# The experts' SiLU written with a hyperbolic tangent in a two-layer kernel on one core

## The reference, cut to what matters

```python
scores = softmax(x @ gate_w); topk_w, topk_idx = top_k(scores, 2)
topk_w = topk_w / (sum(topk_w) + 1e-20)          # w_per_expert: these, spread over the 8 experts
for e in range(8):
    hid = silu(x @ w_gate[e]) * (x @ w_up[e])    # silu(g) = g * sigmoid(g); 128 -> 256 columns
    y = y + w_per_expert[:, e:e+1] * (hid @ w_down[e])
shared = silu(x @ ws_gate) * (x @ ws_up) @ ws_down
return y + shared
```

## Time and profile before

| | us |
|---|---|
| median of 3 runs | 1997.63 (1995.62 to 1999.28) |
| the profiled execution, whole | 1997.42 |
| its span, first to last instruction | 1995.6 |
| TensorE busy / VectorE busy / ScalarE busy | 1638.1 / 1146.3 / 986.9 |
| mean granted TensorE clock | 0.914 of 2.4 GHz |
| ScalarE: ACT_TABLE_LOAD | 100 loads of 1.283 us |

### The profile page before, as it was taken

The page is one execution under the profiler, slowest core; times in us unless marked ns, Lnnn a source line. Parts: engine busy times, 40 slices in busy tenths (PEclk is TensorE's granted clock), DMA queues, the critical chain, the costliest instruction groups (busy, mean ns, idle before and its releaser), DMA issues.

```text
span 1995.6 us, 32820 instructions
## 1 busy us (share of the span) xinstructions
PE 1638.1 (82%) x11632; PEld 956.7 (48%) x11632; DVE 1146.3 (57%) x2565; ACT 986.9 (49%) x2277; POOL 605.0 (30%) x396
## 2 busy tenths in 40 slices
PE   2666569899699978999699978999688988998579
PEld 1334235555446444464546544454445555455235
DVE  6543357557484576557494566646574585744614
ACT  1435253844547544754447535664538445662042
POOL 2624071605242061613324051512515051510000
PEclk9787679999899998999799998999899998999689
DMA  4010011011300122001410123001310123002201
GB/s 131 19 24 1 0 44 41 21 38 44 86 21 2 46 57 65 21 30 32 93 29 5 38 65 64 22 22 32 85 30 21 38 60 68 22 17 61 64 2 53
DMA packets 37333, 80.57 MB, mean 40 GB/s; under 512 B 6782, under 2 KB 22654, under 8 KB 33776
## 3 DMA queue, kind: packets, MB, share of 16 engines
q1 hardware_dynamic: 37152, 78.22, 15.6%
HBM read 54.74 MB, written 8.78 MB: 32 GB/s over the span
## 4 chain that ended last, share of the span: by engine, by line
PE 54%; DVE 16%; ACT 15%; issue 9%; POOL 5%; DMA 1%; DVEq 0%; SPq 0%; POOLq 0%; ACTq 0%
PE ps L350 47%; ACT work L766 8%; PE ps L355 6%; DVE cmax L1116 4%; ACT big L846 4%; POOL small L1237 2%; DVE small L1004 1%; DVE fxn L917 1%; POOL frs L1237 1%; POOL work L1262 1%; DVE x L1198 1%; DVE work L972 1%; POOL work L1273 1%; DVE fst L904 1%; DVE work L971 1%
## 5 line engine op out<-in xcount | busy, mean ns | idle before, releaser
L1262 POOL TENSOR_TENSOR work<-work 128x1024 f32<-128x1024 f32 x64 | 151.0, 2359 | 462.1 <-DVE work L972 461.6
L350 PE MATMUL ps<-bxt,mw 128*128 128x512 f32 x576 | 278.2, 605 | 8.2 <-DVE big L1210 8.2
L350 PE MATMUL ps<-maskb,identb 128*128 128x128 bf16 (+1 forms) x1152 | 237.1, 249 | 47.2 <-ACT work L766 28.2
L766 ACT ACTIVATE work<-ps,pbias,small 128x128 f32<-128x128 f32 x512 | 228.8, 528 | 53.5 <-DVE pbias L1008 53.1
L355 PE MATMUL ps<-ident,work 128*128 128x128 f32 x1056 | 175.2, 313 | 62.7 <-ACT work L766 40.2
L1116 DVE TENSOR_REDUCE cmax<-ps 128x1 f32<-128x384 f32 (+3 forms) x352 | 199.5, 631 | 24.8 <-PE ps L350 24.6
L1237 POOL TENSOR_TENSOR small<-small,consts 128x8 f32<-128x8 f32 x128 | 208.2, 1640 | 5.0 <-DVE small L981 5.0
L350 PE MATMUL ps<-wqkv,h 128*128 128x512 f32 x384 | 188.1, 623 | 23.7 <-ACT v L726 12.0
L1293 POOL TENSOR_TENSOR work<-work,prec 128x1024 f32<-128x1024 f32 x64 | 134.3, 2099 | 209.9 <-DVE prec L999 209.9
L846 ACT ACTIVATE big<-ps 128x512 f32<-128x512 f32 x320 | 167.7, 638 | 58.1 <-PE ps L350 57.8
L868 ACT ACTIVATE big<-ps 128x512 f32<-128x512 f32 x144 | 85.2, 596 | 210.3 <-PE ps L350 209.4
(11 more groups left out here) (163 smaller groups left out, 2600.9 us busy)
## 6 DMA issues: line engine op xcount, KB each, us to landing
mw<-in_experts SPq DMA_DIRECT2D x72, 384.0 KB, 3.1
pk<-scr_parts SPq DMA_DIRECT2D x48, 192.0 KB
pq<-scr_parts SPq DMA_DIRECT2D x144, 64.0 KB
v<-v SPq DMA_DIRECT2D x16, 512.0 KB, 4.5
v<-v SPq DMA_DIRECT2D x16, 384.0 KB, 6.2
scr_parts<-big SPq DMA_DIRECT2D x8, 768.0 KB, 3.7
xin<-in_x SPq DMA_DIRECT2D x8, 256.0 KB, 3.4
out<-x SPq DMA_DIRECT2D x8, 256.0 KB, 6.0
```

What stands on the lines that cost most here:

```text
L350: return nc.tensor.matmul(o, a, b, start=start, stop=stop, skip_group_check=True)
L766: i = nc.scalar.activation(pr[:, m, a, p, :], fb[2 * (m % 2) + a][:, p * P:(p + 1) * P], ACT.Exp, bias=pbias[:, m, k:k + 1], scale=rn[:, m ...
L1262: nc.gpsimd.tensor_tensor(qk[:, m, :], qk[:, m, :], part[m % 2], ALU.add).then_inc(l_add.sem, 1)
```

## The change

The gate's function becomes a tangent on ScalarE. `silu` then holds tanh(g/2). A new step on VectorE, `moe..s`, makes (tanh + 1) · g out of it, in place, from the same PSUM bank. This is twice SiLU. The factor of a half is moved to where it costs no instruction: the sum of the two routing weights is doubled before its reciprocal is taken (one instruction with two operations in place of one), and the shared expert's output is halved in its addition. The semaphore `m_silu` is split into `m_tanh` (ScalarE to VectorE) and `m_gated` (VectorE to TensorE and to its own product), so that a gate's bank is now freed by VectorE. The strings for TensorE, ScalarE and VectorE are new. GpSimd's and SyncE's stay.

```diff
-    "tensor": "FBFBFFFFFFFFFFFFFBBBBFBBBBBBBBBBBBFBBFBBBFBFBBBFFBBBBFBBBBFBBBFBBFBBBFBBBBFBBBBFBBBBBBBBBBBBBBBBBFBB"
+    "tensor": "FFBBFFFFFFFFFFFFFBBBBFBBBBBBBBBBBBFBBBFBBFFBFBBBFBBBBFBBBBFBBBFFBBFBBBBBBBFBBBBFBBBBBBBBBBBBBBBFBFBBF"
...
-        m_silu, m_hid, m_sum = sig("m_silu", ALL * 2), sig("m_hidden", ALL * 2), sig("m_sum", ALL)
+        m_tanh, m_gated = sig("m_tanh", ALL * 2), sig("m_gated", ALL * 2)
+        m_hid, m_sum = sig("m_hidden", ALL * 2), sig("m_sum", ALL)
...
-                                freed = m_hid if q % 2 else m_silu
+                                freed = m_hid if q % 2 else m_gated
...
-                        nc.scalar.activation(silu[e % 2][:, c, :], bb[n % 3][:, :], ACT.Silu).then_inc(m_silu.sem, 1)
+                        nc.scalar.activation(silu[e % 2][:, c, :], bb[n % 3][:, :], ACT.Tanh, scale=0.5).then_inc(m_tanh.sem, 1)
...
-                ts(rs1[:, 3, :], rs1[:, 3, :], 1e-20, None, ALU.add).then_inc(bv.sem, bv.one())
+                ts(rs1[:, 3, :], rs1[:, 3, :], 1e-20, 2.0, ALU.add, ALU.mult).then_inc(bv.sem, bv.one())
...
-                        tt_(outb[:, :, :], bb[3][:, :].rearrange("p (a b) -> p a b", a=NT), outb[:, :, :], ALU.add).then_inc(m_sum.sem, 1)
+                        stt(out=outb[:, :, :], in0=bb[3][:, :].rearrange("p (a b) -> p a b", a=NT), scalar=0.5, in1=outb[:, :, :],
+                            op0=ALU.mult, op1=ALU.add).then_inc(m_sum.sem, 1)
...
+                        yield f"moe{e}{c}s"
+                        n = 4 * e + 2 * c + 1
+                        dve.wait_ge(m_tanh.sem, m_tanh.at(s, 2 * e + c + 1))
+                        stt(out=silu[e % 2][:, c, :], in0=silu[e % 2][:, c, :], scalar=1.0, in1=bb[(n - 1) % 3][:, :],
+                            op0=ALU.add, op1=ALU.mult).then_inc(m_gated.sem, 1)
                         yield f"moe{e}{c}u"
-                        n = 4 * e + 2 * c + 1
                         dve.wait_ge(m_u.sem, m_u.at(s, 2 * e + c + 1))
-                        dve.wait_ge(m_silu.sem, m_silu.at(s, 2 * e + c + 1))
+                        dve.wait_ge(m_gated.sem, m_gated.at(s, 2 * e + c + 1))
```

13 lines of the change are left out of this document (7 added, 6 removed).

## The result

The changed kernel took 1986.37 us, median of 5 runs (1985.36 to 1987.79); the kernel before, in the same set, 1995.93 (1995.10 to 1999.28). The ratio is 0.9949 with a 95% interval of 0.9935 to 0.9964: faster by 0.5%, where no change that can be measured was forecast (1999.5). It lies near the time of rival A (1984.5), and in good part by luck: A had the right place, the start of a turn, but half of its reason did not happen, and the largest part of the gain comes from something that neither the forecast nor a rival named.

A forecast was written before the change was run, and what follows sets the result against it. TensorE, busy 1638.1 of 1995.6 us, hardly stops above the experts. Per turn -1.5 + 2.1 - 0.3 = +0.3, six turns +1.8, last sequence +0.1: 1997.63 with +1.9 gives 1999.5 us, range 1984 to 2012.

The forecast's parts named there:

- rival A: New order wins more: the filled 2.68 us wait passes on, third stretch not held by GpSimd; 1984.5 us, chance 0.28.
- the start of a turn: TensorE's 2.68 us wait for `bxn` is filled, but ScalarE's exponentials end as before: -0.3 us a turn, bound -2.7.
- The loads: 35 activation-table loads leave ScalarE, 44.9 us in all; worth about 0 on the path.
- The products: 144 new VectorE products of 0.69 to 0.75 us each, 99 to 108 us of busy VectorE.
- the second transposes of `fxn`: In the second layer norm, TensorE's wait ahead of these and for the new product would be 2.5 to 3 us.
- the second and third stretch: From the routing through the next sequence's projections, where the experts run: -1.5 us and +2.1 us a turn.
- the last sequence: Run alone at the end: an expert every 5.22 us as now, +0.1 us in all.
- The sum: All terms of a turn added: -1.5 + 2.1 - 0.3 = +0.3 us a turn, six turns +1.8.
- the rest of the first stretch: Local attention and attention of 16 heads, 135.11 us, without experts; only its start was followed, wrong if changed over 0.5.
- a third stretch not held by GpSimd: Part of rival A: projections beside the last experts end earlier, 0.9 of the 2.1 us a turn.

The follow-up runs named there:

- silu_new_opening: Kernel before (SiLU, all loads, old merge) with only the first steps of a turn on TensorE, ScalarE and VectorE in the new order: 1985.0 us.
- silu_new_merge: Changed kernel's whole new order, but with SiLU and its table loads, and the step of the new product empty: 1984.51 us, ratio 0.9938.
- fill_wait: Kernel before with five useless matmuls on TensorE ahead of its wait for `bxn` in every opening, so inside that wait: 1984.09 us.
- fill_behind: Kernel before with five useless matmuls on TensorE in every opening, placed behind its wait for `bxn` instead of in it: 1999.43 us.
- tanh_tensor_opening: Changed kernel with ScalarE's and VectorE's first steps of a turn put back to the old order, TensorE's left new: 1976.94 us.
- tanh_old_opening: Changed kernel with the first steps of a turn on TensorE, ScalarE and VectorE put back to the old order: 1993.73 us.

## Why the prediction was wrong

**The loads, right.** They were put at 0. silu_new_opening has them all, and silu_new_merge too, and both take the changed kernel's time. That they are worth a microsecond or two isn't excluded, since no run takes the loads alone away. The reason given for the tangent needing no load, that it shares a set with the exponential, isn't enough: it stands behind GELU as well, and there too without a load:

```profile
1112.39 0.69 ACT L813 ACTIVATE work<-ps,b 114x512 f32<-114x512 f32 x1 [1.03 <-PE ps L351]
1114.11 0.60 ACT L869 ACTIVATE big<-ps 128x512 f32<-128x512 f32 x1 [1.03 <-PE ps L351]
```

**The products, right.** 0.68 us each. TensorE waits 1.72 us for one of them a turn and no longer for the second transposes of `fxn`, where 2.5 to 3 were forecast for the two, and the second and third stretch together are +0.5 a turn (+0.6 forecast). In the last sequence an expert still takes 5.22 us.

**Where it failed.** The sum had +0.3 a turn and it measured -2.9. Two terms of it are wrong: the start of a turn, and the rest of the first stretch, which had no term at all.

**Start of a turn, the step that failed.** It said: -0.3, since ScalarE would end its exponentials when it did before, with -2.7 as the bound. It measured -1.5 a turn from the first scores to `work,w`, and ScalarE ended the exponentials of the first two blocks some 1.0 us sooner in the turn shown. Two things were wrong in it. The wait was taken for 2.68 us of TensorE's time and no more. It was also what kept the clock low behind it (0.67 over the first 12 us of a turn, 0.83 without the wait), and fill_wait against fill_behind shows that this cost something: 1.4 to some 2 us a turn. And the durations of the new order were taken from rows at the slow clock: 1.99 us for the second block and 2.74 for the projections, where the new order has 1.10 and 1.98. ScalarE's own waits of 2.23, 0.36 and 0.26 for those projections stood in the trace and weren't read; I looked only at its 0.27 behind them. That the other engines' new orders take something back was right in kind: by the medians the two together keep the change some 9 us from what TensorE's order alone gives (tanh_tensor_opening). The part that is seen in the rows is VectorE's.

**The rest of the first stretch, put at nothing.** The prediction said that it had followed only the start of this stretch, and would be wrong if the stretch changed by over 0.5 us; it changed by 3.1. Of the -2.9 a turn, 2.1 are the two drops of the clock behind the opening, the largest single part. fill_behind shows that they go with the timing and not with what was edited, and the 98 merges show with which timing the first of them goes: where the start of `work,w` falls against the clock's beat. The second drop was not examined in this way. A forecast added up from rows doesn't place a turn to half a microsecond. This part is luck, good for the change, and it belonged into the range and not into the mean.

**Rival A** gave the time, with its fill of the wait passing through in part. Its second half, a third stretch not held by GpSimd, did not happen, and the drops of the clock stood in for it. That its time was met is therefore luck in good part.

**Open.** tanh_old_opening keeps 4 us of the gain, more than the same exchange leaves on SiLU's side. Its trace puts them in the pieces with the drops, so I take them for the same effect, but no run separates it from a small worth of the loads.

## What to carry to other kernels

Look at the granted clock in windows of a few us behind every wait of TensorE before pricing the wait: two rows of the same instruction at 1.99 and 1.10 us are the sign, and a step's price in a new order is that of the clock it will meet there. If a wait can't be removed, matmuls that compute nothing can stand in it, but only where a row shows the wait. Before a gain is put down to an edit, look whether it lies in a piece that the edit touches: here two thirds of it didn't. And take each engine's order apart from the others' when a new order is tried: here the best of three was one of them alone.

## What the runs showed of the hardware that was not expected

A wait of 2.7 us, 2.6 us behind a gap of 4.5, kept the clock at 1.2 GHz to about 10 us into the turn, in two turns of five; over the first 12 us of all five the mean granted clock was 0.67. With matmuls in the wait it was 0.83, and in four turns of five the clock was at 2.4 GHz 4 us in. Five matmuls of no use in each opening made the kernel 0.66% faster, 25 of them with a better order 1.9%.

A busy stretch with the same rows ahead of it ran at a granted clock of 1.00 or 0.89 and took 13.9 or 15.6 us, from turn to turn of one execution. In seven merges the slow case came up 0 to 5 times, depending on edits elsewhere, and in 98 merges of 14 traces the place of the stretch against the even beat at which the granted clock changes told slow from fast without exception. The two pieces with such drops differ by up to 16 us over five turns between versions of this kernel (silu_new_opening).

A load of an activation table took 1.28 us. 35 of them fewer, with 144 products more on another engine, changed nothing that could be measured.
